# A sandwich of attention and a low-rank expert mixture on one core: the mixture of a tile runs two tiles behind its output projection, Wo is split where it lands, and tile 1's y begins in slot 33

## What is computed

```python
# x: (4, 512, 1024); 16 heads of 64; everything in float32
x = x + _layernorm(attn(_layernorm(x), Wq, Wk, Wv, Wo))     # rotary, causal softmax, then out @ Wo
x = x + _layernorm(ffn(_layernorm(x), A, B, Wr, br))
# ffn: 8 experts of rank 16
router_logits = jnp.einsum('bsd,hd->bsh', x, Wr) + br
scores = H * jax.nn.softmax(router_logits, axis=-1)
low = jnp.einsum('bsd,hrd->bshr', x, A)
out = SCALING * jnp.einsum('bshr,hor,bsh->bso', low, B, scores)
```

## Time and profile before

| | |
|---|---|
| median of three runs | 1105.83 us |
| the profiled execution, as a run | 1107.44 us |
| its span, first to last instruction | 1105.6 us |
| mean granted TensorE clock in it | 0.995 |
| busy TensorE, VectorE, ScalarE, GpSimd | 97%, 67%, 57%, 40% |
| unit 32 begins on TensorE | 812.0 us |
| y of tile 1 begins | 847.1 us |
| last matmul of y of tile 15 issued | 1079.1 us |

### The profile page before, as it was taken

The page is one execution under the profiler, slowest core; times in us unless marked ns, Lnnn a source line. Parts: engine busy times, 40 slices in busy tenths (PEclk is TensorE's granted clock), DMA queues, the critical chain, the costliest instruction groups (busy, mean ns, idle before and its releaser), DMA issues.

```text
span 1105.6 us, 20082 instructions
## 1 busy us (share of the span) xinstructions
PE 1073.2 (97%) x5556; PEld 886.7 (80%) x5556; DVE 745.4 (67%) x2029; ACT 626.6 (57%) x1437; POOL 438.6 (40%) x413
## 2 busy tenths in 40 slices
PE   7899999999999999999999999999988999999996
PEld 5688787878888888888888888888866888888885
DVE  7677777777666666666666666666665766766676
ACT  6465656566555655555565556555665445455454
POOL 4052524344452625445253543535454233332311
PEclk9999999999999999999999999999998999999999
DMA  6122323231310156021111102112314132323211
GB/s 244 61 80 69 123 66 123 66 124 49 110 49 28 53 181 219 10 72 49 28 53 28 66 9 71 47 29 86 91 48 150 58 113 97 114 87 102 95 58 58
DMA packets 58515, 90.32 MB, mean 82 GB/s; under 512 B 3552, under 2 KB 36320, under 8 KB 58464
## 3 DMA queue, kind: packets, MB, share of 16 engines
q1 hardware_dynamic: 58464, 89.70, 24.8%
HBM read 64.52 MB, written 25.17 MB: 81 GB/s over the span
## 4 chain that ended last, share of the span: by engine, by line
PE 80%; DVE 7%; issue 5%; ACT 5%; DMA 0%; DVEq 0%; POOL 0%; ACTq 0%; POOLq 0%
PE bank L1331 40%; PE bank L1267 29%; PE bank L1358 5%; PE bank L1473 2%; PE bank L1459 1%; PE bank L1309 1%; DVE prob L982 1%; ACT prob L687 1%; DVE q_hl L1014 1%; PE bank L1474 1%; ACT k_hh L713 1%; ACT pT_hi L698 1%; ACT o_low L731 1%; DVE xn L971 1%; DMA xin<-in_x 0%
## 5 line engine op out<-in xcount | busy, mean ns | idle before, releaser
L562 POOL TENSOR_SCALAR prob<-prob,rinv 128x128 f32<-128x128 f32 (+3 forms) x256 | 156.8, 612 | 458.4 <-DVE rinv L992 458.4
L1331 PE MATMUL bank<-big_hi,w_hi 128*128 128x512 f32 x768 | 330.5, 430 | 3.6 <-DVE big_lo L963 3.2
L687 ACT ACTIVATE prob<-prob,nmax 128x128 f32<-128x128 f32 (+3 forms) x256 | 144.0, 562 | 323.1 <-DVE nmax L982 321.9
L1331 PE MATMUL bank<-big_hi,w_lo 128*128 128x512 f32 x768 | 303.3, 395 | 0.0
L1331 PE MATMUL bank<-big_lo,w_hi 128*128 128x512 f32 x768 | 300.8, 392 | 0.0
L1331 PEld LDWEIGHTS bank<-big_hi,w_lo 128*128 128x128 f32 x768 | 144.1, 188 | 33.1
L1331 PEld LDWEIGHTS bank<-big_hi,w_hi 128*128 128x128 f32 x768 | 145.3, 189 | 21.1 <-issue 4.8
L1000 DVE TENSOR_TENSOR pT_lo<-bank,pT_hi 128x128 fp32r<-128x128 f32 (+3 forms) x256 | 123.8, 483 | 54.4 <-ACT pT_hi L698 51.7
L1331 PEld LDWEIGHTS bank<-big_lo,w_hi 128*128 128x128 f32 x768 | 145.8, 190 | 11.3
L982 DVE CUSTOM_DVE_ANT_0 prob<-bank,mask 128x128 f32<-128x128 f32 (+3 forms) x256 | 124.2, 485 | 18.8 <-PE bank L1267 14.5
L992 DVE RECIPROCAL rinv<-rsum 128x1 f32<-128x1 f32 x256 | 40.8, 159 | 134.6 <-ACT prob L687 134.4
(11 more groups left out here) (125 smaller groups left out, 1858.2 us busy)
## 6 DMA issues: line engine op xcount, KB each, us to landing
w_raw<-in_wqkv SPq DMA_DIRECT2D x48, 512.0 KB, 4.2
attention_out<-o_sum SPq DMA_DIRECT2D x64, 128.0 KB, 2.3
xin<-attention_out SPq DMA_DIRECT2D x16, 512.0 KB, 4.7
xres<-in_x SPq DMA_DIRECT2D x16, 512.0 KB, 3.4
out<-res SPq DMA_DIRECT2D x15, 512.0 KB, 2.7
xin<-in_x SPq DMA_DIRECT2D x14, 512.0 KB, 5.3
xT_hold_hi<-xin SPq DMA_DIRECT2D x8, 512.0 KB, 3.6
xT_hold_lo<-xn SPq DMA_DIRECT2D x8, 512.0 KB, 5.4
```

The source lines that it names most:

```text
L562: pool.tensor_scalar(p, p, rinv[:, q % 4:q % 4 + 1], 1.0, ALU.mult, ALU.mult).then_inc(prob_done, 1)
L687: act.activation(prob[:, q % 4, 0:n], prob[:, q % 4, 0:n], ACT.Exp, scale=-1.0, bias=nmax[:, q % 4:q % 4 + 1], accum_out=rsum[:, q % 4:q % ...
L1331: done = pe.matmul(grp_ps[(b + k) % 2][:, :], w, xt, start=at == 0, stop=at == GROUP_MM - 1)
```

## The change

- **Wo.** Chunk c has a place of its own: chunks 0 and 1 land in `xn` and are split into new buffers, chunks 2 to 7 land in the low half of the old xT buffer (`land` lies over `big_lo`) and their low part is written over the raw one. Chunk 0 is split in unit 14, the others in units 30 to 32, all low parts on GpSimd; VectorE splits none.
- **The drain.** Tile 0's y is done in the eight slots of unit 32. The first half of tile 1's y stands in slots 0 to 2 of unit 33 (`Y_SECOND`), its second half behind the last `attend`. Tile 0's first two layernorms stand in unit 33 on VectorE and ScalarE, and so do the splits of A, B and of tile 2's attention output. `xres`, `z`, `xn2` and the B buffers lie in freed parts of older buffers, and the waits of tile 1's y on the last sum of the attention output go (only `low_rank(0)` waits for it).
- **The turns.** Turn t holds y(t) with the whole low-rank part of tile t - 2 between its chunks, in new order, on TensorE, VectorE, ScalarE and GpSimd. Turns 2 to 5 are unrolled, 6 to 13 are the loop, 14 and 15 are unrolled, and behind them stands a tail written out for tiles 14 and 15.

The core of the diff (lines with nothing but "..." mark what is left out):

```diff
-WO_DVE = (4, 6)
-WO_POOL = (0, 1, 2, 3, 5, 7)
-Y_FIRST = (((0, 0), (0, 1), (0, 2)), ((0, 3), (1, 0)), ((1, 1), (1, 2)), ((1, 3),), ((0, 4),), ((0, 5), (1, 4)),
-           ((0, 6), (1, 5)), ((0, 7),), ((1, 6),), ((1, 7),))
-WO_AT = {STEPS * (UNITS - 1) + s: c for s, c in ((0, 0), (1, 1), (2, 2), (4, 3), (8, 4), (9, 5), (10, 6), (11, 7))}
-WO_POOL_AT = {STEPS * (UNITS - 1) + s: c for s, c in ((1, 0), (2, 1), (4, 2), (7, 3), (10, 5), (12, 7))}
-WO_DVE_AT = {STEPS * (UNITS - 1) + s: c for s, c in ((9, 4), (11, 6))}
+Y_FIRST = (((0, 0), (0, 1), (0, 2)), ((0, 3), (1, 0)), ((1, 1), (1, 2)), ((1, 3), (0, 4)), ((1, 4), (0, 5)),
+           ((1, 5),), ((0, 6), (1, 6)), ((0, 7), (1, 7)))
+Y_SECOND = ((0, 1), (2, 3, 4), (5, 6, 7))
+WO_EARLY = UPH - 2
+WO_SLOT = STEPS * (UNITS - 2)
+WO_AT = {STEPS * WO_EARLY + 4: 0} | {WO_SLOT + s: c for s, c in ((4, 1), (9, 2), (10, 3), (12, 4), (13, 5), (18, 6), (19, 7))}
+WO_POOL_AT = {STEPS * WO_EARLY + 6: 0} | {WO_SLOT + s: c for s, c in ((6, 1), (9, 2), (10, 3), (14, 4), (16, 5), (19, 6), (21, 7))}
...
+        sL = ExitStack()
+        spare = sb(sL, "spare", [P, 8192])
+        land = sb(sL, "land", [P, 8192])
+        sL.close()
...
+        wo_own_hi = sb(ctx, "wo_own_hi", [P, 2, EMBED], F32R)
+        wo_own_lo = sb(ctx, "wo_own_lo", [P, 2, EMBED], F32R)
+        wo_hi = [wo_own_hi[:, c, :] for c in range(2)] + [big_hi[:, EMBED * c:EMBED * c + EMBED] for c in range(KC - 2)]
+        wo_raw = [xn[:, c, :] for c in range(2)] + [land[:, EMBED * c:EMBED * c + EMBED] for c in range(KC - 2)]
+        wo_lo = [wo_own_lo[:, c, :] for c in range(2)] + [big_lo[:, EMBED * c:EMBED * c + EMBED] for c in range(KC - 2)]
+        oT = w_raw[:, 0:2, :].rearrange("p i (c t) -> p i c t", c=KC)
...
+                if c == 0:
+                    sp.wait_ge(held, 32 * EARLY + 32)
+                    sp.wait_ge(normed, TILES)
+                elif c == 2:
+                    sp.wait_ge(grp_done, 3 * (UNITS - 1))
+                elif c == 6:
+                    sp.wait_ge(grp_done, 3 * UNITS)
...
+                    if isinstance(u, int) and STEPS * u + s in (STEPS * UNITS - 5, STEPS * UNITS + 6):
+                        oT_low(u - UNITS + 1, u - UNITS + 1)
+                    if isinstance(u, int) and u == UNITS + 1 and s == 2:
+                        oT_low(2, 0)
+                    if isinstance(u, int) and u == UNITS + 1 and s == 3:
+                        pool.wait_ge(bt_hi_done, 1)
+                        pool.tensor_tensor(bt_lo, bt_raw, bt_hi.bitcast(F32), ALU.subtract).then_inc(bt_lo_done, 1)
...
+            def mixed(t, i):
+                pool.wait_ge(normed, ln_third(t) + 1)
+                pool.tensor_tensor(res[:, i, :], res[:, i, :], x1[:, i, :], ALU.add).then_inc(res_done, 1)
+
             def turn(t, i):
-                if tiled(t - 2) and not final(t - 2):
-
-                    pool.wait_ge(normed, ln_third(t - 2) + 1)
-                    pool.tensor_tensor(res[:, i, :], res[:, i, :], x1[:, i, :], ALU.add).then_inc(res_done, 1)
-                if tiled(t + 2) and not (isinstance(t, int) and t >= TILES - 2):
-                    oT_low(t + 2, i)
-
-            turn(0, 0)
-            turn(1, 1)
-            turn(2, 0)
-            turn(3, 1)
-            with pool.Fori(4, TILES - 2, 2) as t:
+                if late(t, 3):
+                    mixed(t - 3, 1 - i)
+                if not final(t):
+                    oT_low(t + 1, 1 - i)
...
+                    if isinstance(u, int) and u == UNITS + 1:
+                        if s == 1:
+                            oT_high(2, 0, 32)
+                        if s == 2:
+                            ln_start(ln_first(0))
+                        if s == 3:
+                            y_normal(0, 0)
+                            act.wait_ge(ffn_in, 32)
+                            act.activation(ar_hi, ar_raw[:, :, :], ACT.Copy).then_inc(ffn_hi_done, 1)
+                        if s == 4:
+                            ln_start(ln_second(0))
+                            x1_normal(0, 0)
+                    if isinstance(u, int) and u == UNITS and s == 5:
+                        act.wait_ge(bt_in, 16)
+                        act.wait_ge(grp_done, 3 * UNITS)
+                        act.activation(bt_hi, bt_raw, ACT.Copy).then_inc(bt_hi_done, 1)
...
             def turn(t, i):
+                x2T_high(t - 2, 0)
+                if late(t, 3):
+                    mixture(t - 3, 1 - i)
+                x2T_high(t - 2, 1)
+                ln_start(ln_first(t - 1))
+                y_normal(t - 1, 1 - i)
+                if not final(t):
+                    oT_high(t + 1, 1 - i, 8 * (t + i) + 16)
+                logits_exp(t - 2)
+                wlT_high(t - 2)
+                ln_start(ln_second(t - 1))
+                x1_normal(t - 1, 1 - i)
+                ln_start(ln_third(t - 2))
...
+            last, before = TILES - 1, TILES - 2
+            mixture(TILES - 3, 1)
+            x2T_high(before, 0)
+            ln_start(ln_first(last))
+            x2T_high(before, 1)
+            act.wait_ge(ln_dve, LN_STEPS * (ln_first(last) + 1))
+            normal(z[:, half(0)], y_ps[1][0][:, :]).then_inc(last_z, 1)
+            act.wait_ge(last_sum, 1)
+            shift(x1[:, 1, half(1)]).then_inc(normed, 1)
+            ln_start(ln_second(last))
+            logits_exp(before)
+            act.wait_ge(ln_dve, LN_STEPS * (ln_second(last) + 1))
+            normal(xn2[:, half(0)], x1[:, 1, half(0)]).then_inc(last_xn, 1)
+            normal(xn2[:, half(1)], x1[:, 1, half(1)]).then_inc(normed, 1)
+            wlT_high(before)
+            x2T_high(last, 0)
+            x2T_high(last, 1)
+            ln_start(ln_third(before))
+            logits_exp(last)
+            wlT_high(last)
+            mixture(before, 0)
+            ln_start(ln_third(last))
+            mixture(last, 1)
...
+                        if s == 1:
+                            y_variance(0, 0)
+                        if s == 3:
+                            ln_scale(ln_first(0))
+                            x1_sum(0, 0)
+                            dve.memset(br_sb[:, 0:HR], 0.0).then_inc(br_zeroed, 1)
+                            dve.wait_ge(x1_done, 1)
+                            layernorm(ln_second(0), [x1[:, 0, 0:512], x1[:, 0, 512:1024]])
+                            dve.wait_ge(ffn_hi_done, 1)
+                            dve.tensor_tensor(ar_lo, ar_raw[:, :, :], ar_hi.bitcast(F32), ALU.subtract
+                                              ).then_inc(ffn_lo_done, 1)
...
             def turn(t, i):
+                dve.wait_ge(y_done, t)
+                half_stats(0, y_ps[1 - i][0][:, :])
+                x2T_low(t - 2, 0)
+                half_stats(1, y_ps[1 - i][1][:, :])
+                ln_variance(ln_first(t - 1))
+                x2T_low(t - 2, 1)
+                ln_scale(ln_first(t - 1))
+                x1_sum(t - 1, 1 - i)
+                low_sum(t - 2)
+                dve.wait_ge(x1_done, t)
+                half_stats(0, x1[:, 1 - i, half(0)])
+                weigh(t - 2)
+                half_stats(1, x1[:, 1 - i, half(1)])
+                ln_variance(ln_second(t - 1))
+                wlT_low(t - 2)
+                ln_scale(ln_second(t - 1))
+                e_stats(t - 2)
+                ln_scale(ln_third(t - 2))
...
+            last, before = TILES - 1, TILES - 2
+            dve.wait_ge(last_y, 1)
+            half_stats(0, y_ps[1][0][:, :])
+            dve.wait_ge(y_done, TILES)
+            half_stats(1, y_ps[1][1][:, :])
+            ln_variance(ln_first(last))
+            x2T_low(before, 0)
+            ln_scale(ln_first(last))
+            dve.wait_ge(xres_in[1], 16 * TILES // 2)
+            dve.wait_ge(res_done, last - 1)
+            scaled_sum(x1[:, 1, half(1)], y_ps[1][1], xres[:, 1, half(1)], ln_first(last))
+            dve.wait_ge(last_z, 1)
+            dve.tensor_tensor(x1[:, 1, half(0)], z[:, half(0)], xres[:, 1, half(0)], ALU.add).then_inc(x1_done, 1)
+            x2T_low(before, 1)
+            dve.wait_ge(x1_done, TILES)
+            half_stats(0, x1[:, 1, half(0)])
+            dve.wait_ge(normed, ln_first(last) + 1)
+            half_stats(1, x1[:, 1, half(1)])
+            ln_variance(ln_second(last))
+            low_sum(before)
+            ln_scale(ln_second(last))
+            weigh(before)
+            x2T_low(last, 0)
+            wlT_low(before)
+            x2T_low(last, 1)
+            e_stats(before)
+            low_sum(last)
+            ln_scale(ln_third(before))
+            weigh(last)
+            wlT_low(last)
...
+                    if isinstance(u, int) and u == UNITS + 1 and s < len(Y_SECOND):
+                        for c in Y_SECOND[s]:
+                            y_half(1, 1, 0, c, c + 1)
...
             def turn(t, i):
-                if final(t - 1):
-                    pe.wait_ge(normed, ln_first(t - 2) + 1)
-                    keep_warm(24)
```

(67 more changed lines are left out.)

329 lines of the change are left out of this document (111 added, 218 removed).

## The result

The changed kernel takes 1115.2 us (median of 4 runs, 1113.67 to 1116.96) against 1105.63 us for the kernel before on the same chip (1105.26 to 1107.13). The ratio is 1.0082, with an interval of 1.0069 to 1.0095: slower by 0.8%. Forecast were 1107.7 us, in a range of 1098.0 to 1112.5. The side is the likeliest of the three that were forecast; the size lies outside the range.

What follows compares the result with a forecast made beforehand. The prediction took TensorE, busy for 97% of the span, as the bound. The seam gives 9.1 us, the turns take back about 8.2 and the end 2.7: 1107.5 us of span, 1107.7 as median, range 1098 to 1112.5.

Steps and rivals of the forecast that it cites:

- What bounds the kernel: Whole kernel: TensorE, busy 97% of the span, sets the time, plus the few places where it waits or runs slowly.
- The seam: Between the two stages: drain filled, clock kept up, turn 2 starting at 852.05 after a 1.15 us wait; gain 9.1 us.
- the 0.3 for a sum held up by GpSimd: At the seam, in tile 0's layernorms: 0.3 us added because GpSimd's `bt_lo` holds up the sum x1.
- The steady turn: In each turn: VectorE delivers `wlow` 0.28 us late for `low_turn` at 9.75; the order alone gives 15.64 us.
- the chain of ten rows: In the turn: durations read from the profile, from the second x2_turn at 2.52 to `wlow` on TensorE at 10.03 us.
- GpSimd and VectorE: In the turn: GpSimd's `oT_low` holds `wlow` until 10.24 - 0.14, making `low_turn` 0.69 us late and the turn 16.05.
- rival 1: In the turns: GpSimd also holds the score ahead of `wlow`; `low_turn` 0.95 late, 3.4 us more, 1111; chance 0.20.
- Turn 15: Last turn: `experts(13)` due at 11.24, `wlT_lo` there only at 11.8, so 16.05 + 0.65 = 16.7 us.
- The end: From the last y to `experts(15)`: 20.2 us where it was 17.5, a loss of 2.7; unchanged behind it.
- rival 2: At the end: the clock falls, `low_rank` and `experts` at 1.2 GHz add some 3 us, 1111; chance 0.10.
- How the numbers followed: Whole kernel: chances faster 0.29, same 0.28, slower 0.43; range from rival 4 to rival 1 with error, 1098 to 1112.5.

Runs made afterwards that it cites:

- no_second: The changed kernel without tile 1's y in unit 33, its 24 matmuls standing behind the last attend instead: 1120.26 us, ratio 1.0119 to the kernel before.
- oT_late: The changed kernel with ScalarE's oT_high moved behind the second layernorm's Ln and Exp, so GpSimd's oT_low lies behind wlow: 1106.31 us, ratio 0.9998 to the kernel before.
- more_warm: The changed kernel with 16 more unused matmuls in the tail: 1114.23 us, ratio 1.0062 to the kernel before.

## Why the prediction was wrong

**What bounds the kernel**: right. TensorE's work is the same, and every us of difference is a wait, a slow clock or a filled drain.

**The seam**: right in kind, 1.4 us late. The clock stayed at 1.00, one wait of 0.59 us stands before the first `x2_turn` (forecast 1.15), and it started at 853.48 (852.05). That is inside the 2 us stated and inside the 851.45 to 855.58 of the other executions. What was late is the start: the chain of tile 0's layernorms takes 8.1 us, as forecast (845.34 to 853.42), but it stands behind the last copy of the probabilities, which ends at 845.42, where the prediction had 843.6; and the 0.3 for a sum held up by GpSimd did not come.

```profile
844.73 0.69 DVE L1023 TENSOR_TENSOR pT_lo<-bank,pT_hi 128x512 fp32r<-128x512 f32 x1 [0.31 <-ACT pT_hi L711]
...
852.18 1.24 ACT L665 ACTIVATE spare<-x,nmr,rstd 128x1024 f32<-128x1024 f32 x1 [0.91 <-DVE nmr L971]
```

Its worth is 7.7 by the prediction's own count, of which `no_second` shows 4 to 5 for slots 0 to 2.

**The steady turn**: the chain of ten rows was good. In turn 3 of the changed kernel the scale, z, the sum x1, `low_sum`, the statistics and `weigh` start at 4.40, 5.27, 6.75, 7.90, 8.63 and 9.23 of the turn, all within 0.01 of the forecast. It put `low_turn` at 10.03 of the turn if nothing is held; `oT_late`, where nothing is held, has it at 10.02 (878.61 - 868.59), and the place where TensorE asks is 9.68, forecast 9.75.

**GpSimd and VectorE**: here is the step that failed. "So `wlow` works only from 10.24 - 0.14" took the hold of the two-input operation as the only one and let the score, one place ahead, pass. The score was held (0.83 for 0.23), `wlow` came behind GpSimd's end at full length, and `low_turn` was 0.94 late, not 0.69. That is rival 1, which priced it at 0.95. It got a chance of 0.20 because its only row was a copy of 64x512 that can take 0.73, and 8 elements were taken for another form. Its 0.25 a turn is 3.3 of the 3.9 us over the 13 turns that have it. The loop, whose turns are 16.43 to 16.54 where 16.15 was forecast, adds 0.9 more, and the other turns 0.1; the loop's part has no experiment. Turn 15 gives 0.4 back (16.29, forecast 16.7): the sum charged it with a hold, but GpSimd has no subtraction in it, and without the hold the prediction's own terms are 15.64 + 0.65 = 16.29.
The Trainium skill (SBUF — State Buffer, § Who interferes with whom) lists tensor_scalar among the forms that can take the pair of ports that VectorE shares with GpSimd, and says that who comes second is blocked fully and for the whole instruction. The traces agree: the score takes 0.83 behind one instruction of 2.48, and score and `wlow` 0.58 and 0.77 behind pieces of 0.73 and 0.72.

**The end**: 20.2 was forecast, 22.44 measured, and two errors hide in that. At full clock it is 19.7 (`oT_late`, `more_warm`), so the order costs 2.2 instead of 2.7. There is a term the sum lacks, since x1's scaled sum waits 0.57 for GpSimd's `mixed(13)` (the bracket at 1087.60), but other links were shorter. The clock took 2.75 on top in the profiled execution: rival 2, whose 3 us was the right size, at a chance of 0.10. This is the second term that the forecast lacked; it had the clock up through the end. The line of x1's sum:

```profile
1087.60 0.75 DVE L1201 SCALAR_TENSOR_TENSOR x<-bank,rstd,land 128x512 f32<-128x512 f32 x1 [0.57 <-POOL res L632]
```

**How the numbers followed**: the range failed too, by a step of its own. Rivals 1 and 2 were treated as alternatives to each other, each ending at 1111, and the range closed at 1112.5. They concern different stretches and nothing in the profile ties them; both came. The forecast with both is 1107.5 + 3.4 + 3 = 1113.9 of span, 1.1 under what was measured. Their joint chance, from 0.20 and 0.10, is small, but the range's upper end should have been the sum of the independent losses beyond the likeliest. Nor is the clock alone to blame for the miss: the two runs at 1113.67 and 1113.72 us lie above 1112.5 as well, since the 1.5 us left above rival 1 were less than the 2 to 3 us of error that the prediction gave the seam and the end.

**Does running behind pay at all?** With the hold gone the changed kernel equals the kernel before (ratios 0.9998 and 0.9997). Stage by stage, `oT_late` has 8.45 us at the seam (861.2 - 852.75), gives back 4.4 in the turns (222.3 against 217.9: 0.31 a turn, about what is waited at `low_turn`) and 2.2 at the end, which leaves the 1.9 us between the spans of the two profiled executions; the medians leave 0.6. No version was found that is faster than the kernel before by more than the measurement can tell.

## What to carry to other kernels

When an order is rewritten, draw the long GpSimd instructions of the new order as bars and ask of every short VectorE operation under them, not only of the two-input ones, whether it can be held; one 8-element operation on the path cost 0.6 us a turn. The cure is to move the start of the GpSimd instruction by moving what releases it; cutting it in pieces only hands the hold to the next operation (here 0.2 us a turn worse). Losses in different stretches add up, so the end of a range is their sum and not the largest of them.
